# Cross-attention with a mixture of experts on one Trainium2 core: spaced indirect transfers, rearranged leftovers, earlier sums

## The reference, cut to what matters

```python
x = x + xattn(layernorm(x), ctx, ctx, W_q, b_q, ..., mask)   # x: 32 batches x 128 rows x 128; 16 heads; ctx: 77 rows
x = x + ffn(layernorm(x), Wp, sim_matrix, temperature, W1, b1, W2, b2)

def ffn(x, ...):                                   # 8 experts, each row goes to 2
    gate_scores = l2norm(x @ Wp.T) @ l2norm(sim_matrix).T / temperature
    top_v, top_i = top_k(gate_scores, 2)
    comb = sum(one_hot(top_i, 8) * softmax(top_v))
    h  = gelu(einsum('bsd,edf->ebsf', x, W1) + b1)          # 128 -> 512
    eo = einsum('ebsf,efd->ebsd', h, W2) + b2               # 512 -> 128
    return einsum('ebsd,bse->bsd', eo, comb)
```

## Time and profile before

| | |
|---|---|
| median of 3 runs | 445.17 us (445.03 to 445.3) |
| the profiled execution | 443.8 us, of which 442.0 us is the span from first to last instruction |
| attention stage | to about 259 us of the span |
| expert stage | about 259 to 421 us: first `eo` at 265.7, last at 420.8 |
| tail | about 421 to 442 us |
| busy share of the span | PE 81%, DVE 70%, ACT 64%, POOL 61% |

### The profile page before, as it was taken

The page is one execution under the profiler, slowest core; times in us unless marked ns, Lnnn a source line. Parts: engine busy times, 40 slices in busy tenths (PEclk is TensorE's granted clock), DMA queues, the critical chain, the costliest instruction groups (busy, mean ns, idle before and its releaser), DMA issues.

```text
span 442.0 us, 13885 instructions
## 1 busy us (share of the span) xinstructions
PE 359.1 (81%) x3564; PEld 299.5 (68%) x3565; DVE 310.4 (70%) x970; ACT 284.6 (64%) x815; POOL 268.3 (61%) x427
## 2 busy tenths in 40 slices
PE   3869888988897889888977878949869999989900
PEld 2447766665675667566755768949769999989900
DVE  5257989888988898889878555635546555556872
ACT  3458887878787878777877465725436565656531
POOL 5623367767686778776863345565655655556673
PEclk9969999999999999999999599978989999999965
DMA  6900001101110101012000032222212222129463
GB/s 172 371 1 5 20 27 40 44 28 33 32 43 24 31 31 43 24 31 82 27 26 14 19 76 56 57 61 63 68 51 67 64 68 61 54 61 264 119 173 113
DMA packets 39052, 29.24 MB, mean 66 GB/s; under 512 B 5107, under 2 KB 34751, under 8 KB 39008
## 3 DMA queue, kind: packets, MB, share of 16 engines
q1 hardware_dynamic: 30592, 18.33, 14.5%
q0 software_dynamic: 4384, 8.60, 6.2%
q10 hardware_dynamic: 4032, 1.77, 1.4%
HBM read 17.53 MB, written 11.62 MB: 66 GB/s over the span
## 4 chain that ended last, share of the span: by engine, by line
PE 59%; DVE 19%; issue 10%; SPq 4%; another core or an unknown queue 2%; DVEq 2%; ACT 1%; DMA 1%; POOL 1%; ACTq 0%; POOLq 0%
PE ps_s L902 14%; PE ps_s L891 13%; PE ps_o L654 8%; PE ps_t L643 6%; PE ps_s L627 5%; DVE rows L1248 5%; DVE sums L1180 3%; SPq L346 3%; PE ps_o L662 2%; PE ps_o L724 2%; PE ps_s L617 2%; PE ps_x L674 2%; DVE pr L1174 2%; DVE cxT L1197 1%
## 5 line engine op out<-in xcount | busy, mean ns | idle before, releaser
L561 POOL DMA_INDIRECT results<-eo,didx x71 | 70.6, 995 | 64.6 <-issue 34.4
L446 POOL DMA_INDIRECT lists<-rows,slots x64 | 65.4, 1021 | 47.8 <-DVE slots L1313 34.1
L891 PE MATMUL ps_s<-xtT,w1c 128*128 128x128 f32 x568 | 78.8, 283 | 7.5 <-DVE xtT L1576 5.5
L948 ACT ACTIVATE pT<-ps_t 77x512 f32<-77x512 f32 x128 | 72.2, 589 | 19.2 <-PE ps_t L643 17.4
L891 PEld LDWEIGHTS ps_s<-xtT,w1c 128*128 128x128 f32 x568 | 70.6, 195 | 12.4 <-DVE xtT L1576 10.0
L902 PE MATMUL ps_s<-w2s,hT 128*128 x568 | 77.5, 281 | 0.6 <-ACT hT L1108 0.4
L643 PE MATMUL ps_t<-identf,pr 128*77 128x128 f32 x512 | 74.5, 286 | 0.0
L902 PEld LDWEIGHTS ps_s<-w2s,hT 128*128 128x128 f32 x568 | 70.4, 195 | 1.2 <-issue 1.0
L1108 ACT ACTIVATE hT<-h 128x512 f32<-128x512 f32 x71 | 44.7, 629 | 39.2 <-PE ps_s L902 25.4
L1104 ACT ACTIVATE w1c<-w1s 128x512 f32 x71 | 44.8, 631 | 34.3 <-PE ps_s L891 16.7
L643 PEld LDWEIGHTS ps_t<-identf,pr 128*77 128x77 f32 x512 | 61.7, 154 | 6.5 <-issue 4.1
(11 more groups left out here) (204 smaller groups left out, 607.6 us busy)
## 6 DMA issues: line engine op xcount, KB each, us to landing
xt<-lists SPq DMA_DIRECT2D x71, 66.0 KB
ys<-results SPq DMA_DIRECT2D x16, 256.0 KB, 4.5
xin<-in_x_dram SPq DMA_DIRECT2D x16, 128.0 KB, 2.2
w1s<-in_L_ffn_W_dram SPq DMA_DIRECT2D x1, 2048.0 KB, 10.0
out_dram<-x ACTq DMA_DIRECT2D x6, 256.0 KB
cin<-in_ctx_dram SPq DMA_DIRECT2D x16, 77.0 KB
results<-eo,didx POOLq DMA_INDIRECT x71
lists<-rows,slots POOLq DMA_INDIRECT x64
```

The source lines that it names most:

```text
L446: nc.gpsimd.indirect_dma_start(lists, bass.IndirectOffsetOnAxis(ap=slots[:, r, s * TOPK + k:s * TOPK + k + 1], axis=0), rows[:, r, s, k, : ...
L561: nc.gpsimd.indirect_dma_start(results, bass.IndirectOffsetOnAxis(ap=didx[:, r:r + 1], axis=0), eo[:, r, :], None, bounds_check=TOPK * NTO ...
L891: last = nc.tensor.matmul(ps_s[:, r, c * P:(c + 1) * P], w1c[:, r, c * P:(c + 1) * P], xtT[:, r, :], start=True, stop=True)
L948: nc.scalar.activation(pT[0:SK, g, :], ps_t[0:SK, g % 2, :], ACT.Copy).then_inc(E[f"t{g}_ready"], 1)
```

## The change

1. **A fill between indirect transfers.** After each transfer of `give_back` POOL fills one of two scratch tiles (`pace`, 128 x 416 float32) with zeros, in turn. Ahead of a transfer POOL waits for the fill of two tiles before.
2. **Leftovers.** Pair 14 is gated and scattered in the attention stage (the bounds `NP - 2` become `NP - 1`; steps 16 to 18 exist on more engines). Pair 15 keeps its place in the expert stage, but at tiles 0 to 8, with one scatter transfer ahead of each of the tiles 8 to 11; its table is made at tiles 9 to 24, one step a tile instead of two.
3. **Loop from tile 27** (`LOOPED` = 27) on PE, ACT and POOL instead of from 31, so that five bodies of 8 loop instead of four; on DVE four bodies, from 27 on.
4. **`EARLY` = 11**: three more batches' sums inside the last tiles.
5. **Tail.** ACT loads chunk 7 itself and stores chunks 0 to 2; SP stores chunks 3 to 7.
6. The two small matmuls that fold the similarity matrix into the gate weights move from ps_x to a free corner of ps_s, one step later; `scatter` issues one transfer a call, `sum_most` has one wait more.

The diff's core. Its first `between` is POOL's and its second PE's; the last bound shown (`gates`) changes in the same way on DVE for `best`, `best_places`, `one_hots`, `chosen`, `chosen_sum`, `chosen_sums`, `ranks`, `rows_of_lists` and `rows_taken`, and on PE for `rank`.

```diff
-    DRAINED = 20
+    DRAINED = 9
+    LOOPED = DRAINED + 18
-    EARLY = 8
+    EARLY = 11
+    LATER = 3
+        pace = sb("pace", [P, 2, 416])
...
-            all_returned(N_TILES)
-            for c in range(PART // CH, NB // CH):
-                load_results(c)
-
-            for c in range(PART // CH, NB // CH):
+            all_returned(sp, N_TILES)
+            load_results(sp, PART // CH)
+
+            for c in range(LATER, NB // CH):
                 store(sp, c)
...
-                if has(J, -2, NP - 2):
-                    scatter(J - 2, m - 2, 1)
+                if has(J, -2, NP - 1):
+                    scatter(J - 2, m - 2, 1, 0)
+                if has(J, -2, NP - 1):
+                    scatter(J - 2, m - 2, 1, 1)
                 if has(J, -1, NP - 1):
                     gate_power(J - 1, m - 1)
...
                 after_tile(pool, FE["eo_ready"], j)
+                after_tile(pool, FE["paced"], j - 2)
                 settled(pool)
...
                                              ).then_inc(returned[r], 16)
+                nc.gpsimd.memset(pace[:, m % 2, :], 0.0).then_inc(FE["paced"], 1)
 
             def between(j):
-                if j == 9:
+                if j == 1:
                     gate_power(NP - 1, NP - 1)
-                elif 10 <= j < 14:
-                    scatter(NP - 2, NP - 2, (j - 10) // TOPK, [(j - 10) % TOPK])
-                elif 21 <= j < 25:
-                    scatter(NP - 1, NP - 1, (j - 21) // TOPK, [(j - 21) % TOPK])
-                elif j == DRAINED + 11:
+                elif 8 <= j < 12:
+                    scatter(NP - 1, NP - 1, (j - 8) // TOPK, (j - 8) % TOPK)
+                elif j == LOOPED:
                     pool.wait_ge(skip_ready, 2)
...
             def between(j):
-                if j == 2:
+                if j == 0:
                     after(pe, E["x2_ready"], NP - 1)
                     turn(NP - 1, NP - 1)
-                elif j == 3:
-                    rank(NP - 2, NP - 2)
-                elif j == 6:
+                elif j == 2:
                     after(pe, E["rk_ready"], NP - 2)
                     gate(NP - 1)
-                elif j == 15:
+                elif j == 7:
+                    after(pe, E["dots_ready"], NP - 1)
                     rank(NP - 1, NP - 1)
...
             act.wait_ge(p_step, 3)
             for c in range(PART // CH):
                 weigh(c)
-            for c in range(PART // CH):
+            all_returned(act, N_TILES)
+            for c in range(PART // CH + 1, NB // CH):
+                load_results(act, c)
+            for c in range(LATER):
                 store(act, c)
...
-                if has(J, -3, NP - 2):
+                if has(J, -3, NP - 1):
                     gates(J - 3, m - 3)
...
-            steps(dve, tile, -3, N_TILES, DRAINED + 11, N_TILES - 4, FRING, between)
+            steps(dve, tile, -3, N_TILES, LOOPED, N_TILES - EARLY - 1, FRING, between)
```

More of the change, by code:

```diff
@@ L259, in after_y, with all_returned, load_results @@
             eng.wait_ge(y_loaded[c], 16 * TOPK)
+        res = results.rearrange("(k c t p) d -> c k p t d", k=TOPK, t=CH, p=P)
+        def all_returned(eng, tiles):
+            for r in range(FRING):
+                eng.wait_ge(returned[r], len(range(r, tiles, FRING)) * 16)
+        def load_results(eng, c):
+            for k in range(TOPK):
+                eng.dma_start(ys[:, c, k, :, :], res[c, k]).then_inc(y_loaded[c], 16)
         def store(eng, c):
@@ L372, in _ @@
             rows_are_there(1, NB)
[L373 to L381, removed]
             late = PART_DONE + FRING + 1
             steps(sp, load_tile, early, late - 1, early, late - 1, FRING)
-            all_returned(PART_DONE)
+            all_returned(sp, PART_DONE)
             for j in range(late, max(N_TILES, late + PART // CH)):
@@ L437, in _, with scatter @@
             pool.wait_ge(headmask4_ready, 1)
-            def scatter(J, m, s, ks=range(TOPK)):
+            def scatter(J, m, s, k):
                 r = m % RING
@@ L544, in _ @@
             step(-1, -1)
-            steps(pool, step, 0, 15, 4, 13)
+            steps(pool, step, 0, 16, 4, 13)
             def places(j, m):
@@ L578, in _ @@
             places(0, 0)
-            steps(pool, give_back, 0, N_TILES - 1, DRAINED + 11, N_TILES - 2, FRING, between)
-            nc.gpsimd.memset(warm[:, :], 0.0).then_inc(all_given, 1)
+            steps(pool, give_back, 0, N_TILES - 1, LOOPED, N_TILES - 2, FRING, between)
+            pool.nop(nofuse=True).then_inc(all_given, 1)
             for c in range(NB // CH):
@@ L803, in step @@
                     keys(J, m)
+                if known(J - 1) and J - 1 == 1:
+                    pe.wait_ge(simt_copied, 1)
+                if known(J - 1) and J - 1 == 2:
+                    pe.wait_ge(wgp_copied, 1)
                 if has(J, -1):
@@ L872, in _ @@
             pe.wait_ge(wpt_copied, 2)
-            steps(pe, step, 1, 17, 6, 14)
+            steps(pe, step, 1, 18, 6, 14)
             pe.wait_ge(tab_ready, 3)
@@ L919, in between @@
                     count_rows(NP - 1, ps_x[:, 0:NE])
-                elif j == DRAINED + 8:
+                elif j == DRAINED + 15:
                     after(pe, E["xn2T_ready"], NP - 1)
                     tables(1)
-                elif j == DRAINED + 11:
+                elif j == LOOPED:
                     pe.wait_ge(tab_ready, 5)
-            steps(pe, tile, -2, N_TILES, DRAINED + 11, N_TILES - 3, FRING, between)
+            steps(pe, tile, -2, N_TILES, LOOPED, N_TILES - 3, FRING, between)
         @block.scalar
@@ L1110, in between @@
             def between(j):
-                if j == 4:
+                if j == 1:
                     turned(NP - 1)
-                elif j == 8:
+                elif j == 3:
                     gated(NP - 1, NP - 1)
-                elif j == DRAINED + 11:
+                elif j == LOOPED:
                     act.wait_ge(tab_ready, 5)
-            steps(act, tile, -2, N_TILES - 1, DRAINED + 11, N_TILES - 3, FRING, between)
+            steps(act, tile, -2, N_TILES - 1, LOOPED, N_TILES - 3, FRING, between)
             act.wait_ge(E["diff_ready"], NP)
@@ L1531, in _ @@
             nc.vector.scalar_tensor_tensor(bo[:, :], bo_row[:, :], anyk[:, 2:3], ps_t[:, 0, 0:D], ALU.add, ALU.add).then_inc(bo_ready, 1)
-            steps(dve, step, 0, 17, 6, 13)
+            steps(dve, step, 0, 18, 6, 13)
             dve.wait_ge(tab_ready, 3)
@@ L1645, in _ @@
             for c in range(EARLY // CH, NB // CH):
-                mine = [b for b in range(c * CH, (c + 1) * CH) if not on_pool(b)]
+                mine = [b for b in range(c * CH, (c + 1) * CH) if b >= EARLY and not on_pool(b)]
                 after_y(dve, c)
```

123 lines of the change are left out of this document (55 added, 68 removed).

## The result

The changed kernel takes 429.56 us (median of 4 runs, 425.74 to 431.32) against 445.21 us (median of 4, 445.03 to 445.3): a ratio of 0.9637, 95% interval 0.9567 to 0.9708. The forecast was 429.2. The time is right; the way to it is only partly so, and the experiments show that most of the gain exists on some chips only.

A forecast was written before the change was run, and what follows sets the result against it. PE bounds the kernel, its notices held while POOL issues transfers 1.3 to 1.4 us apart. Terms -0.6 + 2.2 + 1.0 + 3.0 - 19.1 - 2.5 = -16.0; 443.8 becomes 427.8, median 1.4 higher: 429.2 us, range 421 to 440.

The forecast's parts named there:

- The fill: POOL, between tiles' transfers: 416 elements take 0.40 us, back-to-back transfers 1.78 us apart, so POOL keeps up with PE's 1.90.
- Worth of the even pace: Expert stage: 70 steps at 1.90 us, 133.0 instead of 155.1, -22.1; with four things taken back, -19.1.
- Pair 15's pieces: Expert stage, DVE: pair 15's work, now in tiles 0 to 8, costs +2.1 us.
- where a list transfer stands between two tiles': Tiles 8 to 11: only one of two gaps has the fill, a notice in the other is held; +1.0 us (0 to 5.3).
- slow clock: Expert stage: one fall of PE's granted clock, half a rate over some 3 us of busy time, +1.4 us.
- Four transfers in one row: Ahead of tile 0: pair 14's list transfers without fills hold the notice of the first "up", +3.0 us (0 to 5.3).
- Gating pair 14 ahead of tile 0: Attention stage's end, `x` to first `xtT`: DVE's pieces and a PE trip for `rank` add +2.2 us (1.5 to 3.0).
- turning pair 15: Between the first two "up" groups: waits for DVE's `h` of tile 0 and the second norm, +1.0 us (0 to 2).
- Start: First steps: two similarity matmuls leave the ps_x chain, where PE and ACT wait for one another; -0.6 us (-1.5 to +0.5).
- Tail: After the last tiles: SP stores, fewer sums on DVE, loads from two engines, loads end last; -2.5 us (-4 to +0.5).
- Innocent transfers: Rival, expert stage: notices are late for another cause, so the fill gives nothing; 439.3 us, chance 0.16.
- POOL as the bound: Rival, POOL at each tile: the fill takes longer and the period passes 1.90 us; 463 or 499 us, chance 0.08.

The follow-up runs named there:

- Experiment 11: The change with fills only in tiles 0 to 26, list transfers at tiles 8 to 11 included, none from tile 27: 435.27 us, 0.9636 of before.
- experiment 1: The change without its fill and without the wait for it, on chip 8: 412.48 us, 0.9986 of before.
- experiment 6: The change, unaltered, timed again on chip 8: 413.30 us, 0.9978 of before.
- experiment 8: The change with a fill of twice the size (832 elements), on chip 3: 445.0 us, 0.9874 of before.

## Why the prediction was right, and where it was not

**What bounds the kernel.** Right: PE's notices are held while POOL issues transfers close together, on such chips. Experiment 11 turns both on and off within one run, and on chips without holds the same code shows none. The reading was too narrow: the hold was also in each step of the attention stage, 13.8 us of `cxT`'s waits. And "not held at 1.63 us" was the whole evidence for the distance; experiment 11 bears it out, with the turn between 1.53 and 1.58 us as far as the traces show.

**The fill.** Taken as 0.40 us for 416 elements and 1.78 us from transfer to transfer; measured 0.46 long, of which 0.38 lengthen the distance, 1.76. The extrapolation from three small memsets held. That POOL keeps up: right, busy 120.5 of the 153 us from 257 to 410, where PE has 145.1.

**Worth of the even pace, -22.1 and what was taken back.** From `eo` 16 to `eo` 48 the change takes 61.8 us for 32 steps, 1.93 each, and exactly as much on a chip without holds. Pair 15's pieces: 15.8 us for 7 steps of 1.90 are +2.5, I said +2.1. The failed term is **"where a list transfer stands between two tiles'"**: I took +1.0, with 5.3 as its bound, and +1.4 for a slow clock. `eo` 7 to 16 took 24.8 us where 16.4 were possible, +8.4 for both. One gap in two with a fill gave tiles 8 to 11 the worst of it, since late notices let tiles bunch up, the stall idles PE, and its clock drops to the lower level behind it (0.50 in 296 to 302, showed the same of before). I had priced one hold per gap, by the middle of the loop, though rows 4 showed what list transfers between tiles' do. The stage gained 12.1 instead of 19.1. Counted against nine steps of 1.90, as in the forecast, this stretch has 5.3 of the missing 7.0 us, `eo` 16 to `eo` 48 has 1.0 (61.8 instead of 60.8), and pair 15's pieces and the steps behind `eo` 48 have 0.4 each.

**Four transfers in one row, +3.0.** Wrong: "up" of tile 0 ended inside them and was not held, nor in the two other runs with holds. So closeness alone doesn't suffice. The trace of before has a like case: "up" of tile 16 ends at 299.61, 0.10 inside a transfer that starts 1.34 us behind the one before, and the copy follows at 299.77. All four groups ran at the lower clock (2.08 us for the three and 1.93 for this one, instead of 1.06). Whether that is what spared them is open.

**Gating pair 14 ahead of tile 0, +2.2, and turning pair 15, +1.0.** Measured +2.0 and, to `eo` 0, +2.0 (on chip 8 +1.9 and +1.3). The first is right, the second within its bounds (0 to 2), at the upper one.

**Start, -0.6.** The trace gives -3.4. 1.6 of them come in the last step alone, where PE's granted clock was 0.65 in before (242.7 to 257.0) and 0.88 after: luck, not the edit, as far as the runs show, for the last step takes 10.8 us in experiment 1 and 12.0 in experiment 6, whose attention stages are the same. On chip 8 the start is no shorter in the change (244.3 against 243.6); up to `x` of pair 14 it is 0.4 shorter there (232.35 against 232.76), near the forecast.

**Tail, -2.5.** Measured -1.1. The waits went as forecast, and the loads end last. From the last transfer's end to the end of the span it is 16.9 instead of 18.7 us; the last transfer starts 2.2 us behind the last `eo` instead of 1.5. The sums behind the landing took 4.0 us where I had 3 to 3.5, and the last store landed 6.3 us after the sums instead of 5.4.

**The sum.** -3.4 + 2.0 + 2.0 - 12.1 - 1.1 = -12.6, against my -16.0. That the median met 429.2 within 0.4 us has a second reason: I set the median 1.4 above the profiled execution, as in before, but the profiled one of the change was the longest of four, 1.8 above the median. The changed kernel scatters over 5.6 us, the old one over 0.3. The two runs with the higher mean clock (0.958) are the two faster ones; so I take the stall and the clock behind it for the cause, which was not shown.

**The rivals.** *Innocent transfers* falls on chips with holds; on those without, its premise is true, and there is nothing to win. I had cited for it the Trainium skill (SBUF — State Buffer, Who interferes with whom), that PE and ACT never wait at the SBUF ports. Experiment 1 agrees: beside a busy POOL, Gelu came 0.10 us after "down". No run shows ports at work in the holds either. *POOL as the bound* was placed right and priced a little high: experiment 8 had a period of 2.11, 0.21 above 1.90, for which the prediction's price is 14.7 us; its ratio to before is 0.024 above the change's, some 10.5 us, on another chip. No rival said that the gain depends on the chip, and no view of one trace could.

## What to carry to other kernels

Where GpSimd issues indirect transfers beside a pipeline of TensorE, look at how far apart they start and how late the readers of PSUM go on; a short fill (here 0.38 us) behind each costs little as long as GpSimd has slack against the bound (on chip 8 0.9 us of 413 in the change, and 2.9 where it was added to the kernel before, whose list transfers took up the slack), and half a measure (one gap in two) leaves a stall of the old size. Before building on a stall that one trace shows, time the kernel on a second chip: here before differed by 31 us of 445 between two chips, and the same change is worth 3.6% on one chip and 0.2% on another. Where two conditions can be put into two parts of one execution, as in experiment 11, the chip drops out of the comparison.

## What the runs showed that was not expected

The kernel before takes 414 us on chips 8, 6 and 1, and 445 to 451 on the first chip, 3 and 13; each session had one level only, and the traces differ in late notices of PE and the lower clock that follows a stall. Whether it lies in the chip or in what surrounds it is open. Where notices are held, pairs of transfers 1.38 to 1.48 us apart hold them mostly by 1.0 to 1.4 us (0.6 at the least), and rows 1.30 to 1.40 apart by up to 6 us; but not the row ahead of tile 0 and not "up" of tile 16. At 1.52 to 1.53 us Gelu still comes 0.7 to 1.4 late. Where all gaps are 1.62 us or more it is at most 0.7, which the traces without holds show too (0.66 at tile 24 of experiment 1). After a pair 1.38 apart the hold ends 0.5 to 0.8 us behind the second transfer's end.
